# Attention passes: row of indices, attention vector and forward scan kept in a PSUM bank, sums through a ring of three banks

## The reference, cut to what matters

```python
# layer 0 (pass l0; 4 heads of 32)
e = leaky_relu(x_l[src] + x_r[dst], 0.2)
logits = einsum('ehc,hc->eh', e, att)
m = segment_max(logits, dst)
p = exp(logits - m[dst])
alpha = p / (segment_sum(p, dst)[dst] + 1e-16)
out = segment_sum(x_l[src] * alpha[:, :, None], dst)
# layer 2 (pass l2; 8 heads of 16)
att = sum(Q[row] * K[col], axis=-1)        # per head
alpha = segment_softmax(att, row)
out = segment_sum(V[col] * alpha[:, :, None], row)
```

## Time and profile before

| | us |
|---|---|
| median of 3 runs | 9281.45 (9280.75 to 9319.1) |
| profiled execution, span from its first to its last instruction | 7912.9 |
| time of the profiled execution beyond its span | not in the profile |
| POOL busy in it | 5523.4 (70%) |
| PE, DVE, ACT busy | 4838.3, 4476.8, 2097.8 |
| pass l0, first to last gather issue | 1455.2 to 2681.6 |
| pass l1, the same | 2877.2 to 3934.8 |
| pass l2, the same | 4079.9 to 5340.0 |

### The profile page before, as it was taken

How to read it: one execution, slowest core, us unless ns; L and a number is a source line. 1 busy time by engine, 2 the same in 40 slices (tenths; PEclk the granted TensorE clock), 3 DMA queues, 4 the chain that set the end, 5 groups by cost and what they waited for, 6 DMA issues and landing times. The chain is left out here.

```text
span 7912.9 us, 112109 instructions
## 1 busy us (share of the span) xinstructions
PE 4838.3 (61%) x32954; PEld 3963.3 (50%) x32954; DVE 4476.8 (57%) x15028; ACT 2097.8 (27%) x4735; POOL 5523.4 (70%) x5311
## 2 busy tenths in 40 slices
PE   4799887666666547777656566664555556444442
PEld 3466665566556446666635455553444444333332
DVE  9999998677777653333346666665444443111113
ACT  9454443122222241111121111112232223111110
POOL 0477777577777557777757788774777774777775
PEclk9999999788888755555577766766565558555555
DMA  0122221566666446666557766762555553333333
GB/s 15 32 56 55 53 53 35 157 162 161 158 162 160 107 87 134 134 136 134 127 149 203 205 198 200 207 197 66 156 156 156 156 156 87 99 104 104 105 104 80
DMA packets 1304014, 990.39 MB, mean 125 GB/s; under 512 B 287713, under 2 KB 1192995, under 8 KB 1303411
## 3 DMA queue, kind: packets, MB, share of 16 engines
q0 software_dynamic: 183088, 352.33, 18.0%
q1 hardware_dynamic: 700995, 378.63, 17.1%
q10 hardware_dynamic: 419328, 252.26, 11.6%
HBM read 613.75 MB, written 368.79 MB: 124 GB/s over the span
## 5 line engine op out<-in xcount | busy, mean ns | idle before, releaser
L983 POOL DMA_INDIRECT l_rows<-tab,by_src x1664 | 1813.0, 1090 | 611.0 <-issue 506.6
L983 POOL DMA_INDIRECT l_rows<-tab,by_dst x832 | 974.0, 1171 | 324.8 <-issue 237.2
L983 POOL DMA_INDIRECT l3a_rows<-tab,by_dst x832 | 804.4, 967 | 297.1 <-issue 253.3
L983 POOL DMA_INDIRECT l3b_rows<-tab,by_dst x832 | 793.5, 954 | 294.4 <-issue 253.2
L802 POOL DMA_INDIRECT sorted_dst<-pay,place_i x783 | 792.3, 1012 | 275.3 <-issue 237.8
L1129 PE MATMUL l_ps_z<-l_win,l_sel_t 128*128 128x128 f32 x3328 | 758.0, 355 | 204.6 <-DMA l_rows<-tab,by_dst 178.3
L1430 PE MATMUL l3b_ps_o<-l3b_rows,l3b_sel 128*128 128x128 f32 x1664 | 425.7, 437 | 631.3 <-DMA l3b_rows<-tab,by_dst 631.3
L1129 PEld LDWEIGHTS l_ps_z<-l_win,l_sel_t 128*128 128x128 f32 x3328 | 609.8, 251 | 227.9 <-issue 171.6
L1430 PEld LDWEIGHTS l3b_ps_o<-l3b_rows,l3b_sel 128*128 128x128 f32 x1664 | 370.5, 328 | 686.9 <-issue 686.9
L1430 PE MATMUL l3a_ps_o<-l3a_rows,l3a_sel 128*128 128x128 f32 x1664 | 402.2, 417 | 484.5 <-DMA l3a_rows<-tab,by_dst 484.5
L1457 DVE TENSOR_SCALAR l3b_sel<-iota,by_dst 128x128 f32<-128x128 f16 x832 | 186.1, 303 | 859.3 <-PE l3b_ps_o L1430 855.7
(11 more groups left out here) (423 smaller groups left out, 12349.8 us busy)
## 6 DMA issues: line engine op xcount, KB each, us to landing
parts<-l_sums ACTq DMA_DIRECT2D x416, 264.0 KB
l_win<-win SPq DMA_DIRECT2D x1664, 64.0 KB
parts<-l3a_sums SPq DMA_DIRECT2D x208, 512.0 KB, 3.0
l_row<-slot_rows ACTq DMA_DIRECT2D x624, 128.0 KB, 3.2
parts<-l_sums ACTq DMA_DIRECT2D x208, 272.0 KB, 4.0
parts<-l3b_sums SPq DMA_DIRECT2D x208, 256.0 KB, 2.4
low_bc<-lo_rows SPq DMA_DIRECT2D x194, 256.0 KB
l_rows<-tab,by_src POOLq DMA_INDIRECT x1664
```

The lines of the kernel that those rows point to most:

```text
L983: pool.indirect_dma_start(rows[:, q, g, :], None, table, bass.IndirectOffsetOnAxis(ap=index[:, k * G + g:k * G + g + 1], axis=0))\
```

## The change

The two banks of each `ps_o` become a ring of three tiles of one bank each, of which a group uses two: each half of a group (2 tiles of edges) has its own matmuls, its own semaphore count and its own ACT copy. One of the 8 banks is thereby freed. It becomes `ps_own`, which DVE alone uses: the row of indices (now fp32), the attention vector, and the result of the forward scan `prefix`. The first two are copied there once at the start of the pass. The copy of the two ends of `top` moves from DVE to ACT, behind the exponential, and gets a semaphore `edge_done` for which `top` waits. `l_ps_own` is the name of the new tile in the listings below.

```diff
+OP = 3
...
-        prefix = kit.sb(f"{name}_prefix", [hg, 2, P])
...
-        ps_o = [kit.ps(f"{name}_ps_o{i}", [P, 2, 512]) for i in range(2)]
+        ps_o = [kit.ps(f"{name}_ps_o{i}", [P, 2 * w]) for i in range(OP)]
+        ps_own = kit.ps(f"{name}_ps_own", [P, G, P])
+        iota, att, prefix = ps_own[:, 0], ps_own[:, 1], ps_own[0:hg, 2]
...
 @block.tensor
                     pe.wait_ge(val_done, j + 1)
-                    wait_count(pe, sums_done, j - 1)
-                    for g in range(G):
-                        mm = pe.matmul(ps_o[j % 2][:, g // 2, g % 2 * w:(g % 2 + 1) * w], sel[:, j % 3, g],
-                                       val[:, j % 2, g], start=True, stop=True)
-                    mm.then_inc(sums_ps, 1)
+                    for h in range(2):
+                        m = 2 * j + h
+                        wait_count(pe, sums_done, m - OP + 1)
+                        for i in range(2):
+                            mm = pe.matmul(ps_o[m % OP][:, i * w:(i + 1) * w], sel[:, j % 3, 2 * h + i],
+                                           val[:, j % 2, 2 * h + i], start=True, stop=True)
+                        mm.then_inc(sums_ps, 1)
...
 @block.scalar
-                    act.wait_ge(sums_done, j + 1)
+                    act.wait_ge(sums_done, 2 * j + 2)
                     act.dma_start(part_rows(c, w, j), sums[:, j % OB]).then_inc(stored[j % OB], 16)
...
-                    wait_count(act, sums_ps, j - 1)
+                    wait_count(act, sums_ps, 2 * j - 2)
                     act.activation(val[:, j % 2, :, D:w], ps_p, ACT.Copy).then_inc(weight_done, 1)
                 if 0 <= k - 4 < GROUPS:
                     j = k - 4
-                    act.wait_ge(sums_ps, j + 1)
                     wait_count(act, stored[j % OB], 16 * (j // OB))
-                    act.activation(sums[:, j % OB].rearrange("p (i g) w -> p i (g w)", i=2),
-                                   ps_o[j % 2][:, :, 0:2 * w], ACT.Copy).then_inc(sums_done, 1)
+                    for h in range(2):
+                        m = 2 * j + h
+                        act.wait_ge(sums_ps, m + 1)
+                        act.activation(sums[:, j % OB, 2 * h:2 * h + 2].rearrange("p g w -> p (g w)"), ps_o[m % OP],
+                                       ACT.Copy).then_inc(sums_done, 1)
...
                     act.activation(weight[:, j % 2], diff[:, j % 2], ACT.Exp).then_inc(exp_done, 1)
+                    act.activation(c.edge_top[0:hg, j], top[:, j % 2, 0::P - 1], ACT.Copy).then_inc(edge_done, 1)
...
 @block.vector
+            dve.tensor_copy(iota, c.iota16[:, 0:P]).then_inc(homed, 1)
+            if not dot:
+                dve.tensor_copy(att, c.att[:]).then_inc(homed, 1)
...
-                    dve.tensor_tensor_scan(prefix[:, j % 2], run[:, j % RB, 0:P], ps_s, -BIG, ALU.add, ALU.max)\
+                    dve.tensor_tensor_scan(prefix, run[:, j % RB, 0:P], ps_s, -BIG, ALU.add, ALU.max)\
...
-                    dve.tensor_tensor_scan(top[:, j % 2, ::-1], run[:, j % RB, P:2 * P][:, ::-1], prefix[:, j % 2, ::-1], -BIG,
+                    wait_count(dve, edge_done, j - 1)
+                    dve.tensor_tensor_scan(top[:, j % 2, ::-1], run[:, j % RB, P:2 * P][:, ::-1], prefix[:, ::-1], -BIG,
...
-                                      replicate(c.att[:], 1, G), ALU.mult).then_inc(prod_done, 1)
+                                      replicate(att, 1, G), ALU.mult).then_inc(prod_done, 1)
...
-                    wait_count(dve, sums_ps, j - 2)
-                    dve.tensor_tensor(sel[:, j % 3], replicate(c.iota16[:, 0:P], 1, G),
+                    wait_count(dve, sums_ps, 2 * j - 4)
+                    dve.tensor_tensor(sel[:, j % 3], replicate(iota, 1, G),
...
-                if 0 <= k - 2 < GROUPS:
-                    j = k - 2
-                    dve.tensor_copy(c.edge_top[0:hg, j], top[:, j % 2, 0::P - 1])
```

More of the change, by code:

```diff
@@ L1080, in attention_pass @@
              "diff_done", "exp_done", "weight_ps", "weight_done", "val_done", "sums_ps", "sums_done", "masks",
-             "bounds"))
+             "bounds", "homed", "edge_done"))
         landed, landed_before = c.pool_dma, list(c.pool_count)
@@ L1184, in _ @@
                 carry_masks(dve, c, key, masks)
+            dve.wait_ge(homed, 1 if dot else 2)
             for k in range(-1, GROUPS + 4):
```

2 lines of the change are left out of this document (1 added, 1 removed).

## The result

| | before | after |
|---|---|---|
| median of 5 runs each, us | 9284.06 (9280.75 to 9320.32) | 9462.23 (9440.85 to 9519.0) |
| ratio | 1 | 1.0194, 95% interval 1.0164 to 1.0224 |

The change makes the kernel 1.9% slower; forecast were 8965 us and a range of 8865 to 9110. In words for what follows: the *ring* is the sums in halves through three banks, the *homes* are the iota row, the attention vector and the scan in `ps_own`.

A forecast was written before the change was run, and what follows sets the result against it. POOL's gathers, held by DVE instructions with two SBUF inputs, were taken to bound l0 and l2. Fewer holds would save 141 us in l0 and 175 in l2, together 316: 9281 - 316 = 8965 us, range 8865 to 9110.

The forecast's parts named there:

- The holds, who causes them, and that they go: l0 and l2: DVE instructions with two SBUF inputs hold gathers; PSUM inputs free them, a group falling to 5.22 us.
- Rival B: Gathers of l0 and l2: two SBUF inputs are not what holds a gather, so no gain, 9281 us; chance 0.05.
- The prices on VectorE and ScalarE: l0 and l2: PSUM accesses add 0.1 us an iteration on DVE, half copies 0.17 on ACT; all hidden, cost 0.
- Rival C: DVE in l0 and l2: each PSUM access costs +0.65 us, so the kernel is 148 us slower, 9429; chance 0.03.
- POOL never pauses, so POOL sets the end of both passes: l0 and l2: waits for `val` sum to 16.2 us and nothing, so gather time alone counts; 141 and 175 us saved.
- The median lies 1368.6 above the span, and I take that as unchanged: Whole kernel: the span's saving of 316 us comes off the median in full, 9281 to 8965.
- The alternative that I worked out: Whole kernel: unprofiled execution slower all over by 1.173, so the gain would be 371 us, giving 8910.
- If it falls and POOL now waits for `val`: Sign of being wrong in l0 and l2: the gathers' mean falls, yet POOL waits for DVE's `val`.
- l2's chain: In l2: `ps_o`, copy, exponential, transpose, `ps_z`, `ps_o` took 5.03 us, should fall to 4.8; the next bound there.
- the second price of rival A: l2 limited by transfers at 207 GB/s: l2 gains 24 us and l0 141, giving 9116; the rival's chance 0.11.

The follow-up runs named there:

- e1: The kernel before, unchanged, profiled again for a trace beside the changed kernel's; ratio 0.9998 to before.
- e3: The changed kernel with ring and all homes, but the ends of `top` copied by DVE as before; ratio 1.0219 to before.
- e2: The changed kernel with the ring only: homes undone and the ends of `top` copied by DVE again; ratio 1.0013 to before.
- e5: e2 with only the iota row in PSUM, attention vector and scan in SBUF; ratio 1.0243 to before.
- e11: e3 with gathers of l0 and l2 after the first eight groups fetching 128 bytes a row, from wrong rows; ratio 1.0258 to before.
- e13: e3 where in l0 and l2 later groups reuse the first four groups' rows and gathers go to slots nobody reads; ratio 1.1292 to before.
- e15: e3 with DVE making `sel` a second time, from SBUF, into a tile nobody reads; ratio 1.0091 to before.
- e14: e2 where in l0 and l2 later groups reuse the first four groups' rows and gathers go to slots nobody reads; ratio 1.1296 to before.

## Why the prediction was wrong, step by step

**The holds, who causes them, and that they go.** Right. The gathers' means fell to 974 and 990 ns, forecast 0.98 to 1.02 us, and the unchanged l1 kept its time (1204.7 us in e1, 1203.8 in e3). The Trainium skill's inference ("SBUF — State Buffer", Who interferes with whom) that `tensor_tensor` leaves descriptor generation alone is contradicted once more: taking one of the two inputs of `sel` out of SBUF took the mean from 1131 (e2) to 1006 ns (e5). Rival B fell with it.

**The prices on VectorE and ScalarE.** Right, and hidden: `prod` 649 where 0.65 stood, `top` 395, `sel` 672; the halves of the sums 391 ns each, forecast 0.39; `edge_top` on ACT 187 ns. Rival C forecast slower, but by a price of 0.55 us or more for each access, and that isn't there; its l2 would have been faster. I had the sign in the rivals and not the mechanism.

**"POOL never pauses, so POOL sets the end of both passes."** This is the step that failed. It was read from a trace in which it holds, and carried to runs in which it doesn't. Every microsecond of holds that went was to come off the passes, 141 us of l0 and 175 of l2. Measured from e2 to e3, l0 grew by 67 us and l2 by 77. POOL's time in a group of l0 shows what came in place of the holds. It is 5.04 us of its own, plus what it is held, plus what it waits; that is bookkeeping, and holds whatever the cause. e2 has 0.73 held and 0.73 waiting: 5.04 + 1.46 = 6.50 (measured 6.55, 1356.4 / 207). e3 has 0.14 and 1.65: 5.04 + 1.79 = 6.83 (6.88). The homes took 0.59 us of holds away, and 0.92 us of waits for `val` came in their place, with TensorE's results late more often. The term that the prediction put at nothing without a reason is this one: what a gather that isn't held does to TensorE.

**"The median lies 1368.6 above the span, and I take that as unchanged."** It was the warning that I passed over. A gap of 15% between the times and the only trace means that the trace isn't one of those executions. Nothing was outside the span: e1 has 9189.0 inside, l0 of 1347.0 us where the first trace has 1213.0 by the same two instructions, and l1 as told above. The alternative that I worked out, everything slower by one factor, was wrong too, since the extra time is one of interference and changes with the holds.

**"If it falls and POOL now waits for `val` (C or l2's chain)."** The sign that I named came, but not for the reasons named. Of the range, the second price of rival A, 9116, lay outside the 9110 that was said to include it; nothing hangs on that.

**What stays open.** Why TensorE gets on better for several short holds than for one long wait (1.46 us a group of held and waiting time with the holds, 1.79 without) was not isolated. A hold falls where VectorE works and so where TensorE has work; a wait for a full ring falls where both have stopped. That is an argument, not a measurement. What POOL's gathers and TensorE's instructions share was not found either. The bytes of a row (e11) and late landings (e13) are excluded; the work of issuing a gather and the moving of its 128 rows are left, and no run separates them. Why TensorE gets through one instruction per gather in e13 and many more in e3 is open too. And why the first trace is free of it can't be told from here.

## What to carry to other kernels

Compare the span of the trace with the timed runs before anything is read from it; where they differ by more than a few us, the trace may have another bound than the runs, and no saving may be priced from it. An engine that seems to be held up by another may be giving a third one its only time: ask who advances while it is held, and give the hold back in an otherwise equal kernel, as e15 does, to see what it is worth. Where GpSimd's indirect gathers run back to back beside fp32 products, count TensorE's instructions before making the gathers faster; taking 16 of 52 away was the only edit here that made the kernel faster with its whole work done, if by 0.27% only.

## What the runs showed of the hardware that I had not expected

- In e13 and e14 TensorE gets through about one instruction, a weight load or a matmul, per indirect gather while GpSimd issues these without a pause: 1.405 and 1.408 us an instruction beside a gather every 1.406 us (e13), in two passes with 52 and 36 instructions a group. It is not so everywhere: in e3's short groups 52 instructions go beside three gathers in 4.53 us, and the first trace has no such delay at all. The Trainium skill ("SBUF — State Buffer", the same section) says of the SBUF's ports "PE and ACT never wait on anyone". As a rule for TensorE's time it fails in e13; whether the wait is on a port of the SBUF, no run here shows.
- TensorE's recorded times don't show this. Its matmuls stand in the trace 46 us ahead of the first consumer in e13, and up to 26 us in e1. The sign is a consumer that waits for "remote" or "issue" in groups whose product has long been recorded.
- In the same stretch of e13 a gather takes 1.07 us in place of 0.95, with hardly a VectorE instruction beside it.
- One input of one instruction (`sel`) moved to PSUM took most of the holds of `top` and `prod` away too: 1006 ns in e5, 990 with all three.
- Without gathers, TensorE's granted clock is 1.00 in l0 and 0.95 in l2, against 0.82 and 0.72 in e1's stretches, with less idle time between its products; the kernel is 10% faster, 8256.29 us.
